# An image tower with one normalisation chain at its opening, and its last eight tiles taken by channel halves, tiles and pairs

## The reference

```python
h = patches @ tok_W                                       # 768 -> 256
n = layernorm(h)
mod = gelu(n @ mod_w1 + mod_b1) @ mod_w2 + mod_b2          # 256 -> 1024 -> 256
m = (n @ in_w + in_b) * mod
y = irfft(rfft(m) * rfft(kernel))                          # along the 196 tokens, per channel
h = h + y @ out_w + out_b
n = layernorm(h)
base = n @ base_W.T + base_b;  shared = (n @ shared_A.T) @ shared_B.T
gate = softmax(n @ router_W.T + router_b)                  # 6 experts
w = top-2 of gate, divided by (their sum + 1e-6)
routed = sum_e w[e] * ((n @ routed_A[e].T) @ routed_B[e].T)   # rank 16
out = h + base + shared + routed
```

## Time and profile before

| | us |
|---|---|
| median of three runs | 1251.4 (1250.5 to 1251.81) |
| the profiled execution | 1251.14 |
| its span in the trace | 1249.4 |
| outside the span | 1.7 |
| first projection starts | 30.06 |
| second projection starts | 58.29 |
| last sum starts | 1246.05 |

### The profile page before, as it was taken

One profiled execution on the slowest core, in us unless ns is written; L12 is line 12 of the kernel. 1 busy time (PEld: TensorE's weight loads), 2 busy tenths in 40 slices (PEclk: granted clock), 3 DMA queues, 4 the chain that ended last, 5 costly groups with the idle time before them and its releaser, 6 DMA issues.

```text
span 1249.4 us, 21119 instructions
## 1 busy us (share of the span) xinstructions
PE 1226.5 (98%) x8163; PEld 1200.4 (96%) x8163; DVE 861.1 (69%) x2557; ACT 587.9 (47%) x1110; POOL 404.2 (32%) x463
## 2 busy tenths in 40 slices
PE   5999999999999999999999999999999999999997
PEld 5999999999999999999999999999999999999986
DVE  6467676677666677666677666677666677666676
ACT  5644454444454444454444444444444444444432
POOL 4622332322332322332322332322332322332310
PEclk9999999999999999999999999999999999999999
DMA  7111111011111011111011111011111011110001
GB/s 244 39 39 52 51 48 42 16 49 52 51 44 46 14 51 51 52 42 48 14 52 51 52 39 51 14 52 51 52 39 51 14 52 51 52 39 16 14 13 34
DMA packets 23470, 57.26 MB, mean 46 GB/s; under 512 B 2825, under 2 KB 18506, under 8 KB 19402
## 3 DMA queue, kind: packets, MB, share of 16 engines
q1 hardware_dynamic: 22554, 55.13, 12.7%
q10 hardware_dynamic: 816, 0.79, 0.2%
HBM read 43.07 MB, written 12.85 MB: 45 GB/s over the span
## 4 chain that ended last, share of the span: by engine, by line
PE 95%; DVE 3%; ACT 1%; POOL 0%; DMA 0%; issue 0%; DVEq 0%; POOLq 0%
PE rotating L1237 17%; PE rotating L1239 17%; PE rotating L1238 17%; PE rows_ps L1237 10%; PE rows_ps L1238 10%; PE rows_ps L1239 10%; PE turn L1480 5%; PE turn L1464 2%; PE turn L1276 2%; PE rows_ps L1285 2%; PE turn L1237 1%; PE turn L1238 1%; PE turn L1239 1%; PE rotating L1345 1%; POOL w_l L434 0%; DMA prod<-dram_tok_w 0%
## 5 line engine op out<-in xcount | busy, mean ns | idle before, releaser
L575 ACT ACTIVATE gelu<-rotating,biases 128x392 f32<-128x392 f32 x256 | 149.1, 583 | 203.6 <-PE rotating L1239 203.5
L468 POOL TENSOR_TENSOR folded<-modulated 128x196 f32<-128x196 f32 x63 | 38.1, 604 | 558.0 <-DVE modulated L979 558.0
L455 POOL TENSOR_TENSOR gelu_l<-gelu,gelu_h 128x784 fp32r<-128x784 f32 x62 | 117.4, 1894 | 223.4 <-DVE norm L962 197.4
L440 POOL TENSOR_TENSOR patches_l<-patches,patches_h 128x384 fp32r<-128x384 f32 x186 | 184.8, 1023 | 0.3 <-ACT patches_h L533 0.3
L1237 PE MATMUL rotating<-gelu_h,w_h 128*128 128x392 f32 x512 | 177.7, 347 | 0.0
L1237 PE MATMUL rotating<-x_h,w_h 128*128 128x392 f32 x512 | 177.2, 346 | 0.0
L1239 PE MATMUL rotating<-x_h,w_l 128*128 128x392 f32 x512 | 174.7, 341 | 0.0
L1238 PE MATMUL rotating<-x_l,w_h 128*128 128x392 f32 x512 | 174.6, 341 | 0.0
L1238 PE MATMUL rotating<-gelu_l,w_h 128*128 128x392 f32 x512 | 174.3, 340 | 0.0
L1239 PE MATMUL rotating<-gelu_h,w_l 128*128 128x392 f32 x512 | 174.0, 340 | 0.0
L1237 PE MATMUL rows_ps<-tokw_h,patches_h 128*128 128x256 f32 x576 | 165.3, 287 | 7.6 <-POOL patches_l L446 7.6
(11 more groups left out here) (259 smaller groups left out, 2922.8 us busy)
## 6 DMA issues: line engine op xcount, KB each, us to landing
patches<-dram_x_rest SPq DMA_DIRECT2D x31, 1152.0 KB, 5.1
out<-h_sb SPq DMA_DIRECT2D x30, 384.0 KB, 2.9
patches<-dram_x_first SPq DMA_DIRECT2D x3, 384.0 KB, 5.1
h_sb<-dram_x_second SPq DMA_DIRECT2D x1, 768.0 KB, 8.4
prod<-dram_tok_w ACTq DMA_DIRECT2D x2, 256.0 KB, 5.6
gelu<-dram_w SPq DMA_DIRECT2D x1, 512.0 KB, 6.7
out<-h_sb SPq DMA_DIRECT2D x1, 512.0 KB, 2.9
out<-h_sb SPq DMA_DIRECT2D x2, 256.0 KB, 2.2
```

Source lines behind the costliest of these rows:

```text
L440: pool.tensor_tensor(patches_l[:, k, :], patches[:, k, :], patches_h[:, k, :].bitcast(F32), ALU.subtract).then_inc(pool_patches_lo, 1)
L455: pool.tensor_tensor(gelu_l[:, 2 * j:2 * j + 2, :], gelu[:, 2 * j:2 * j + 2, :], gelu_h[:, 2 * j:2 * j + 2, :].bitcast(F32), ALU.subtract)\
L468: pool.tensor_tensor(folded[:, m, 0, :, 1:NF], fwd, back, ALU.add)
L575: act.activation(gelu[:, k, :], bank(g + 1, UP[k])[:, 0:GT], ACT.Gelu, bias=b1_bias[:, k:k + 1]).then_inc(act_gelu, 1)
```

## The change

Opening. The embedding weights are now issued by SP too, alternating with the patches, in pieces of 1, 1, 2 and 2 k-blocks (`CHUNKS`). A third intake (tile 5) follows in_w, and a fourth (tiles 6 and 7) takes the place of the first full one; out_bias and the shared weights move back in the queue. DVE makes all low parts of the first tiles and of in_w; POOL makes those of w1 only. Tiles 0 to 3 form one intake with one normalisation chain; ACT applies it to two tiles, DVE to two. Tiles 4 (three products) and 5 (plain float32 products on the unsplit weights) are embedded before the first projection; tiles 6 and 7 in round one. The first projection goes by input halves. w2's split is spread over round one on ACT, the split of the fourth intake stands between two of its gelus, and the shared products move to the end of round one. TensorE begins with seven products on a row of ones; ACT begins with a gelu on three zeros, with which its function table is loaded.

End. The last down-product is not interrupted any more, the last spectrum goes by channel halves (one half combined by POOL, one by DVE, each with an inverse DFT and a y of its own), the exponential stands between the two sine copies, the gate takes its ranks from the logits and multiplies tile by tile with one reciprocal, the second quad is transposed, copied, turned and finished by pairs, and of thirteen clock-keeping products three are left.

```diff
+CHUNKS = ((0, 1), (1, 2), (2, 4), (4, 6))
...
 def intake_tiles(r):
-    return ((0, 1, 2), (3, 4))[r] if r < 2 else (3 * r - 1, 3 * r, 3 * r + 1)
+    return {0: (0, 1, 2, 3), 2: (4, 5, 6, 7)}[r] if r < 3 else (3 * r - 1, 3 * r, 3 * r + 1)
...
+            for n, (a, b) in enumerate(CHUNKS):
+                sp.dma_start(tokw_wait[n], blocks(tok_w)[:, a:b, :]).then_inc(tok_w_in[n], 16)
+                sp.dma_start(patches[:, a:b, :], x_first[:, a:b, :]).then_inc(first_in[n], 16)
...
             weight("in_w")
+            sp.dma_start(third, x_third).then_inc(third_in, 16)
...
             weight("w1")
+            sp.dma_start(out_bias[:, :], out_bias_d).then_inc(out_bias_in, 16)
             load_patches(2)
+            sp.dma_start(biases[:, :], biases_d).then_inc(biases_in, 16)
             weight("w2")
...
+            def split_w1():
+                pool.wait_ge(weight_hi, ORDER.index("w1") + 1)
+                for src, waiting, hi, lo in splits["w1"]:
+                    pool.tensor_tensor(lo, waiting, hi.bitcast(F32), ALU.subtract).then_inc(w1_lo, 1)
...
+            def half_spectrum():
+
+                pool.wait_ge(quad_ones_row, 1)
+                pool.wait_ge(dve_half_spec, 1)
+                for x, op in ((0, ALU.subtract), (1, ALU.add)):
+                    pool.tensor_tensor(channels(spec_y, x, 0), channels(spec_y, x, 0), channels(prod, x, 0), op)\
+                        .then_inc(pool_half_spec, 1)
...
-            normalise(0, 0)
+            first_normalise()
+            first_x1_hi()
...
             ins.then_inc(spectrum_ready, 1)
-            x1_hi(0)
-            normalise(1, 1)
-            x1_hi(1)
-            split_hi("w2")
-            patches_hi(2)
+            split_w2_hi((0,))
...
+                    split_w2_hi((1, 2))
                 gelu_tile(mid, 0)
                 gelu_tile(mid, 1)
-                gelu_hi(mid, 0)
+                if i == 1:
+                    patches_hi(2)
...
-            quad_normalise(0, (2, 3))
-            quad_tokens_out(0)
+            first_quad_tokens_out()
+            act.wait_ge(pe_idft, DH * last + 1)
+            y_sine_half(0)
             quad_exp(0)
-            y_sine(last)
+            act.wait_ge(pe_idft, DH * last + 2)
+            y_sine_half(1)
             last_y_hi()
             first_quad_gated_out()
-            quad_normalise(1, (3,))
-            quad_tokens_out(1)
+            quad_normalise(1, (2, 3))
+            last_quad_tokens_out()
...
                 dve.wait_ge(pe_dft, GROUPS + 1)
-                dve.tensor_tensor(prod[0:NF, 0, :], turn[0:NF, 1, :], spec_k[:, 1, :], ALU.mult)
-                dve.tensor_tensor(spec_y[0:NF, 1, :], turn[0:NF, 1, :], spec_k[:, 0, :], ALU.mult).then_inc(dve_spec, 1)
+                dve.tensor_tensor(p_re, x_im, k_im, ALU.mult)
+                dve.tensor_tensor(y_im, x_im, k_re, ALU.mult).then_inc(dve_half_spec, 1)
+                if m == 1:
+                    dve.wait_ge(dve_half_spec, 2)
+                    dve.tensor_tensor(y_re, y_re, p_re, ALU.subtract)
+                    dve.tensor_tensor(y_im, y_im, p_im, ALU.add).then_inc(dve_half_spec, 1)
...
+                room, n = quad_rooms[q], QUAD
+                e4 = [P, n, EXPERTS, EXPERTS]
+                logits = room.wide[:, 0]
+                dve.wait_ge(dve_gate, GATE_STEPS * (GROUPS - 2) + QUAD_GATE * q + 3)
+                other = logits.rearrange("p t (a e) -> p t a e", a=1).broadcast_to(e4)
+                own = logits.rearrange("p t (e a) -> p t e a", a=1).broadcast_to(e4)
+                quad_link(q, 4, dve.tensor_tensor(room.cmp[:, 0], other, own, ALU.subtract))
+                flat = lambda c: room.cmp[:, c].rearrange("p t e f -> p (t e f)")
...
+                room = quad_rooms[q]
+                small = lambda c: room.small[:, c]
+                wide = lambda c: room.wide[:, c].rearrange("p t e -> p (t e)")
                 dve.wait_ge(act_quad_exp, q + 1)
-                gate(GATE_STEPS * (GROUPS - 2) + QUAD_GATE * q + 3, quad_routes[q], quad_rooms[q])
-
...
+                for t in range(QUAD):
+                    hidden = quad_routes[q][:, t, 0:ROUTED].rearrange("p (e r) -> p e r", r=RANK)
+                    chosen = room.wide[:, 4, t, :].rearrange("p (e a) -> p e a", a=1).broadcast_to([P, EXPERTS, RANK])
+                    dve.scalar_tensor_tensor(out=room.gated[:, t, :].rearrange("p (e r) -> p e r", r=RANK),
+                                             in0=hidden, scalar=room.small[:, 5, t:t + 1], in1=chosen, op0=ALU.mult,
+                                             op1=ALU.mult).then_inc(dve_tile_gated, 1)
+
...
-            keep_h(0)
+            split_inw()
             stats = stats1(0)
-            layer_norm_scales(0, stats, slice(0, 1), 3)
-            keep_h(1)
-            stats = stats1(1)
-            layer_norm_scales(1, stats, slice(1, 2), 2)
-            x1_lo(0)
-            x1_lo(1)
+            layer_norm_scales(0, stats, slice(0, 2), 2)
+            first_normalise()
+            keep_first_h((3, 0))
+            first_x1_lo()
+            keep_first_h((1, 2))
...
+            layer_norm_scales(GROUPS, stats, slice(0, 2), 2)
+            modulate(last, 1)
+            last_fold()
             quad_normalise(0, (0, 1))
             last_fold_lo()
-            last_products()
-            spectrum_of_y(last)
+            half_products(0)
+            half_products(1)
             quad_logits(0)
-            whole_y(last)
+            whole_y_half(0)
+            quad_ranks(0)
+            whole_y_half(1)
             last_y_lo()
-            quad_gate(0)
+            quad_weights_of(0)
             quad_mixer(1, 1, 0)
             quad_stats(1, 1, 0)
...
-            layer_norm_scales(GROUPS + 2, stats, slice(0, 2), 2)
-            quad_normalise(1, (0, 1, 2))
-            quad_finish(0)
+            layer_norm_scales(GROUPS + 1, stats, slice(0, 2), 2)
+            quad_normalise(1, (0, 1))
+            last_quad_tokens_out()
+            quad_finish(0, 0)
+            quad_finish(0, 1)
             quad_logits(1)
-            quad_gate(1)
-            quad_gated_out()
-            quad_finish(1)
+            quad_ranks(1)
+            quad_weights_of(1)
+            quad_gated_rows(1)
+            last_quad_gated_out()
+            quad_finish(1, 0)
+            quad_finish(1, 1)
 
         @block.tensor
...
+            def second_tile(n, ps):
                 for k in range(KT):
-                    if k % 2 == 0:
-                        pe.wait_ge(pool_first_lo, KT // 2 + k // 2 + 1)
-                    else:
...
+            def third_tile(ks):
+
+                for k in ks:
+                    ins = pe.matmul(next_rows[1], third[:, k, :], tokw_f[k], start=False, stop=k == KT - 1,
+                                    skip_group_check=True)
+                return ins
...
+            keep_clock(rotating[:, 2], 7, ones)
+            first_tiles()
+            second_tile(0, first_rows[3]).then_inc(pe_embed, 1)
+            second_tile(1, next_rows[0])
+            pe.wait_ge(setup_in, 16 * SETUP_LOADS)
+            spectrum_products()
+            pe.wait_ge(third_in, 16)
+            third_tile((0, 1))
             pe.wait_ge(ident_in, 16)
-            spectrum_products()
             turn_x1(0)
-            shared_products()
-            pe.wait_ge(dve_x1_lo, 1)
-            turn_x1(1)
+            third_tile(range(2, KT)).then_inc(pe_embed, 1)
...
             first_quad_out()
-            mlp_down(last, 1, range(2, HC))
+            mlp_down(last, 1, range(HC))
             pe.wait_ge(dve_y, DH * last)
             free = rotating[:, 1]
             pe.wait_ge(dve_mod, DH * last + 1)
             keep_clock(free, 2)
             last_turn_fold()
-            keep_clock(free, 5)
+            first_quad_turn_x2()
+            keep_clock(free, 1)
             last_dft()
-            quad_turn_x2(0)
-            keep_clock(free, 1)
-            quad_routes_products(0)
-            keep_clock(free, 1)
-            inverse_dft(last)
+            first_quad_routes()
             quad_base_products(0, (0,))
+            pe.wait_ge(pool_half_spec, 2)
+            last_inverse_dft(0)
+            pe.wait_ge(dve_half_spec, 3)
+            last_inverse_dft(1)
             pe.wait_ge(dve_mod, DH * last + 2)
             last_quad_out()
             quad_base_products(0, (1, 2))
             pe.wait_ge(dve_quad_h, 3)
-            quad_turn_gated(0)
+            for t in range(QUAD):
+                ins = quad_turn_gated(0, t)
+            ins.then_inc(pe_quad_turned, 1)
             quad_base_products(0, (3,))
-            quad_routed(0)
-            keep_clock(rows_ps[:, 1], 2)
-            quad_turn_x2(1)
-            quad_routes_products(1)
+            pe.wait_ge(quad_weights, 3)
+            pe.wait_ge(quad_ones_row, 1)
+            pe.wait_ge(act_quad_gated, 1)
+            for t in range(QUAD):
+                ins = quad_routed(0, t)
+                if t % 2 == 1:
```

(17 more changed lines are left out.)

529 lines of the change are left out of this document (329 added, 200 removed).

## The result

The changed kernel took 1241.88 us (median of four executions, 1239.86 to 1242.16), the kernel before 1251.06 beside it: ratio 0.9922, 95% interval 0.9909 to 0.9935. It is 9.2 us faster; 12.3 were forecast. The profiled execution took 1241.79 us for a span of 1240.0, beside 1251.14 before.

A forecast was written before the change was run, and what follows sets the result against it. TensorE, busy 98% of the span, was taken as the bound, leaving gains only at both ends. Opening 8.6 and end 3.7 us off 1251.14 gave 1238.8 us; own range 1236.8 to 1240.8, overall 1235.8 to 1243.

The forecast's parts named there:

- they cost nothing to drop as long as the clock stays up: End: the ten removed clock-keeping products only fill TensorE's idle time, so dropping them costs nothing if the clock holds.
- Rival (1): Clock lower than taken: 1.6 us more in the opening, 3 us at the end, 1241.8 us; chance 0.15.
- (a): End: down-product quarter moved, spectrum by halves, table load between the sine copies; second sine copy earlier, 0.6 us gained.
- (b): End: DVE's gate between y and the mixer's sum shortened, ranks moved ahead into a wait; 2.2 us gained.
- (c): End: four row products of 96 columns now stand between the two sums; 0.8 us lost.
- (d): End: DVE normalises two tiles, not three, and tokens are copied by pairs on two engines; 0.6 us gained.
- (e): End: second gate shortened from 4.25 to 3.1 us, but TensorE is in its base products for 3.64; 0.6 us gained.
- (f): End: turn, copy, product and last sum go by pairs, 2.7 instead of 3.2 us; 0.5 us gained.
- w1 is there at about 16.4: Opening: 0.23 MB more ahead of w1 at 364 GB/s costs 0.6 us; the four tiles' normalisation chain runs 17.5 to 18.5.
- Rival (2): Round one: w1 or w2 comes 2 to 4 us late through ACT or a DMA, 1241 to 1243 us; chance 0.14.
- (3): End: ACT drains before the table load, 1.4 us on the second sine copy, 1240.2 us; chance 0.04.
- (5): Slower: w2 landing late delays ACT's split and TensorE's second up-product; landing at 39 gives 1253.9 us; chance 0.03.

The follow-up runs named there:

- after again: The changed kernel run once more without an edit; median 1240.36 us, ratio 0.9916.
- The run with two queues: Embedding weights issued by ACT instead of SP, against the changed kernel with clock-keeping products added at both ends; median 1241.83 us.
- The third-intake run: Third intake (393 KB) queued behind w1, against the changed kernel with clock-keeping products added at both ends; median 1240.26 us.
- pieces of two: Embedding weights and first patches in pieces of 2, 2 and 2 k-blocks, against the changed kernel with clock-keeping products at both ends; median 1241.21 us.

## Why the prediction came out as it did

The mechanism and its places were right; 1238.8 was 3.1 us under the median, inside the range and outside the likeliest case's own 1236.8 to 1240.8. The sum was missed in two steps: by 1.25 us in the opening (7.35 for 8.6) and by 1.73 at the end (1.97 for 3.7).

**The step that failed at the end: "they cost nothing to drop as long as the clock stays up".** The clock was this step's condition, and it went down in the profiled execution and, by their times, in half of all eight. Rival (1) had its price nearly right (1.6 us a fall, measured 1.65 at the end). That its time, 1241.8, fits the measured 1241.88 is luck: it added two falls, and there was one, with the other 1.3 us lost to the opening's lateness. Its chance of 0.15 was too little. My reason against it, a clock of 0.99 over the old end, came from a single profile. By its own signs the forecast was wrong in the first profile, twice: a granted clock of 0.5 behind 13 us, and the last addition 1.97 us, so within 2, from its old distance.

With the clock up ("after again") the six terms can be read at the same distances, forecast in brackets: (a) second sine copy 0.67 (0.6); (b) 2.21 (2.2); (c) -0.89 (-0.8), the four row products in 0.97; (d) to the routes 0.37 (0.6); (e) to the turn of gated rows 0.94 (0.6); (f) 0.32 (0.5). Sum 3.62 for 3.7. What was read off rows of the same operation came within 0.1; (d) to (f), estimates over several engines, are off by 0.2 to 0.3 with changing signs, so that the sum fits better than its terms is luck.

**The step that was mis-sized in the opening: "w1 is there at about 16.4" and the chain "to 18.5".** w1 came at 17.66 and DVE's chain ended at 19.3, so the first projection came at 23.25, not 22.2. I had carried over 364 GB/s from the old stretch behind 12.9 us, though bytes had to be counted from the start: between 4 and 8 us the one queue moved 273 GB/s, the old two 407. The run with two queues brought w1 0.73 us earlier, a little over half of the 1.26 us by which it was late; the rest stays open. The third-intake run shows that w1 was the smaller half: the chain stands right behind. It began late since patches came late: the last subtraction of the second intake ended at 14.6, not 13.5. The cover I had named for DVE's work, w1's arrival, was as thin as the thing it covered.

From the first to the second projection 27.69 us were measured and 27.5 forecast, by luck, since the errors cancel: projection -1.43 (-1.6), the up-products with ACT's stalls +0.92 (+1.5, of which only 0.48 shows as a wait), shared +1.06 (+1.1), embedding -1.78 (-2.05), the rest with four tiles' normalisation +0.69 (+0.35).

Right were also: 384 columns on DVE alone in 0.56 us (0.5 taken), the warm-up products as a minor term, and no drain ahead of the table load: in "after again" the copy starts at 1213.80, the load at 1214.15 and the exponential at 1215.45. Rival (2) came in part: w1 was 1.3 us late, below its 2 to 4. Rivals (3), (4) and (5) did not occur; w2's split waited 1.10 us for its DMA at 24.63, and TensorE did not stand for it.

What stays open: why the clock falls in one execution and not in the next of the same program. The runs show only that it does, with waits equal within 0.02 us, and that with the wait filled it fell in none of eight profiles.

## What to carry to other kernels

Where a kernel ends in short pieces of TensorE work, price its waits with a possible fall of the clock behind them, and fill them with products nobody reads: five in a wait of 1.38 us cost nothing, and the spread went from 2.3 to 0.9 us. They do not calm the opening: the kernels with pieces of two and without the warm-up carried the five too and still spread over 2.1 and 1.65 us. Judge such a change by the traces' distances, since its median depends on how many executions happened to fall. When a late transfer and a chain of small instructions meet at one point, work out both arrivals before giving either a price: here moving the transfer by 0.5 us was worth nothing.
